# Layout in DRAM of the split q and k of two attention stages: loads by head, one store in place of four

## The reference, cut to what matters

```python
# self attention, 16 heads of 16 features, T = 256
q, k = apply_rotary(q), apply_rotary(k)
weights = softmax(einsum('bhqd,bhkd->bhqk', q, k) * SCALE)
# cross attention: two softmaxes of half heads (8 features), S = 120 keys
a1 = softmax(einsum('bhtd,bhsd->bhts', q1, k1) * SCALING)
a2 = softmax(einsum('bhtd,bhsd->bhts', q2, k2) * SCALING)
attn = einsum('bhts,bhsd->bhtd', a1 - lam * a2, v) * (1 - LAMBDA_INIT)
```

## Time and profile before

| | before |
|---|---|
| median of three runs | 1919.88 us |
| the profiled execution | 1924.67 us |
| its span in the profile | 1922.6 us |
| mean granted clock of TensorE | 0.946 |
| TensorE busy, weight loads | 88%, 62% |
| VectorE, ScalarE, GpSimd busy | 68%, 56%, 45% |
| DMA packets | 312,751, 302.79 MB |
| queue of SP's transfers, share of 16 engines | 62.0% |

### The profile page before, as it was taken

One profiled execution on the slowest core, in us unless ns is written; L12 is line 12 of the kernel. 1 busy time (PEld: TensorE's weight loads), 2 busy tenths in 40 slices (PEclk: granted clock), 3 DMA queues, 4 the chain that ended last, 5 costly groups with the idle time before them and its releaser, 6 DMA issues. The chain is left out here.

```text
span 1922.6 us, 43658 instructions
## 1 busy us (share of the span) xinstructions
PE 1690.0 (88%) x14562; PEld 1183.5 (62%) x14562; DVE 1310.4 (68%) x2959; ACT 1083.8 (56%) x1701; POOL 858.5 (45%) x788
## 2 busy tenths in 40 slices
PE   3789999999999997889989989999898749999985
PEld 2566667666666665555556555555555438888774
DVE  3566776777666775668888887988888544444275
ACT  1466666666666665567777777777776501111244
POOL 4567776777666742211212111111211005887565
PEclk6899999999999999899999999999998759999998
DMA  5577767776777666566655566566664326887686
GB/s 121 132 190 184 193 168 196 188 188 170 195 189 188 169 172 144 123 119 132 139 132 128 127 129 125 136 133 141 135 125 87 90 59 177 197 195 196 178 292 218
DMA packets 312751, 302.79 MB, mean 157 GB/s; under 512 B 68842, under 2 KB 289836, under 8 KB 303304
## 3 DMA queue, kind: packets, MB, share of 16 engines
q1 hardware_dynamic: 302408, 288.66, 62.0%
q0 software_dynamic: 10240, 12.81, 3.9%
HBM read 188.36 MB, written 112.00 MB: 156 GB/s over the span
## 5 line engine op out<-in xcount | busy, mean ns | idle before, releaser
L1340 DVE TENSOR_REDUCE att_nmax<-self_p_mx 128x2 f32<-128x512 f32 x512 | 328.8, 686 | 203.3 <-PE self_p_mx L629 202.8
L1430 DVE TENSOR_REDUCE att_cross_nmax<-self_p_mx 128x8 f32<-128x960 f32 x256 | 294.4, 1150 | 86.5 <-PE self_p_mx L829 85.4
L1074 ACT ACTIVATE att_probs<-self_p_sc 128x1024 f32<-128x1024 f32 x256 | 261.3, 1021 | 98.5 <-PE self_p_sc L617 96.2
L1167 ACT ACTIVATE att_probs<-self_p_sc 120x1024 f32<-120x1024 f32 x256 | 261.9, 1023 | 65.4 <-PE self_p_sc L811 64.5
L629 PE MATMUL self_p_mx<-att_k_stack,att_q_stack 96*128 96x256 bf16 x1024 | 160.8, 277 | 54.5 <-DMA att_k_stack<-self_k_parts 49.2
L847 PE MATMUL self_p_pv<-att_probs,att_v_aug 120*32 120x256 f32 x2048 | 172.3, 410 | 0.0
L617 PE MATMUL self_p_sc<-att_q_stack,att_k_stack 99*128 99x256 bf16 x1024 | 158.5, 278 | 11.4 <-ACT att_probs L1074 10.0
L829 PE MATMUL self_p_mx<-att_k_stack,att_q_stack 48*128 48x120 bf16 x2048 | 101.2, 220 | 70.6 <-DMA att_k_stack<-cross_k_parts 37.9
L1683 POOL TENSOR_SCALAR att_cross_var_eps<-att_cross_mv 128x2 f32<-128x2 f32 x32 | 7.2, 226 | 332.3 <-DVE att_cross_mv L1536 289.7
L1697 POOL TENSOR_TENSOR att_qk_rest<-att_qk,att_parts 128x752 f32<-128x752 f32 x32 | 51.8, 1619 | 214.3 <-ACT att_parts L1200 214.3
L629 PEld LDWEIGHTS self_p_mx<-att_k_stack,att_q_stack 96*128 96x128 bf16 x1024 | 96.0, 98 | 82.9 <-DMA att_k_stack<-self_k_parts 35.3
(11 more groups left out here) (180 smaller groups left out, 3682.4 us busy)
## 6 DMA issues: line engine op xcount, KB each, us to landing
att_q_stack<-self_q_parts SPq DMA_DIRECT2D x64, 256.0 KB, 5.7
expert_sums<-att_zeros SPq DMA_DIRECT2D x64, 256.0 KB, 8.7
att_q_stack<-cross_q_parts SPq DMA_DIRECT2D x128, 128.0 KB
ffn_w<-in_ffn_w SPq DMA_DIRECT2D x64, 256.0 KB
ffn_m_sb<-expert_sums SPq DMA_DIRECT2D x32, 512.0 KB, 6.0
self_q_parts<-att_parts SPq DMA_DIRECT2D x32, 384.0 KB
self_k_parts<-att_parts SPq DMA_DIRECT2D x32, 384.0 KB
att_k_stack<-self_k_parts SPq DMA_DIRECT2D x32, 384.0 KB, 7.9
```

The source lines that it names most:

```text
L1074: act.activation(probs[:, g % 4, :], p_sc[:, :, :].rearrange("p b n -> p (b n)"), ACT.Exp, scale=SCALE).then_inc(s_exp, 1)
L1167: act.activation(probs[0:KEYS, g % 4, :], p_sc[0:KEYS, :, :].rearrange("p b n -> p (b n)"), ACT.Exp, scale=C_SCALE).then_inc(c_exp, 1)
L1340: dve.tensor_reduce(nmax[:, M.slot, :, m], p_mx[:, m % 2, :].rearrange("p (c k) -> p c k", c=TC), AX_X, ALU.max, negate=True).then_inc(s_r ...
L1430: dve.tensor_reduce(cnmax[:, M.slot, :, :, 2 * m:2 * m + 2].rearrange("p c e h -> p e h c"), p_mx[:, :, 0:4 * KEYS].rearrange("p e (x k) - ...
```

## The change

The self parts in DRAM get rows of `T + 32` = 288 values (576 B) of which 256 are used, so that the 16 head rows of one feature don't follow each other without a gap, and the stack loads name the head as a dimension of its own: 16 pieces of 512 B per row. The cross parts of q and k of both half heads lie in one tensor whose rows are the 752 values (1504 B) of a partition of `cparts`: one transfer stores all of them, and the stack loads take 512 B (q) or 240 B (k) of each row. The counts on `c_pw` go from 64 to 16 a batch. Number, order and bytes of the stack loads stay as they were.

```diff
--- before.py
+++ after.py
@@ -141,8 +141,9 @@
     y_rows = y_out.rearrange("(b c p) d -> b p c d", p=P, c=TC)
     moe_rows = [m[0:N_TOK, :].rearrange("(b c p) d -> b p c d", p=P, c=TC) for m in moe]
     res_rows = res_out.rearrange("(b c p) d -> b p c d", p=P, c=TC)
-    q_dram = nc.dram_tensor("self_q_parts", [3, NP, 2, P, T], BF16, kind="Internal").ap()
-    k_dram = nc.dram_tensor("self_k_parts", [3, NP, 2, P, T], BF16, kind="Internal").ap()
+    PITCH = T + 32
+    q_dram = nc.dram_tensor("self_q_parts", [3, NP, 2, P, PITCH], BF16, kind="Internal").ap()
+    k_dram = nc.dram_tensor("self_k_parts", [3, NP, 2, P, PITCH], BF16, kind="Internal").ap()
 
     C_LAGS = 7
     KEYS = ctxT_in.shape[1]
@@ -176,8 +177,7 @@
     cres_rows = res_out.rearrange("(b c p) d -> b p c d", p=P, c=TC)
     ctxT_rows = ctxT_in.rearrange("(b f p) n -> b p f n", f=FC, p=P)
     cy_rows = z_out.rearrange("(b c p) d -> b p c d", p=P, c=TC)
-    cq_dram = nc.dram_tensor("cross_q_parts", [3, E, NP, P, T], BF16, kind="Internal").ap()
-    ck_dram = nc.dram_tensor("cross_k_parts", [3, E, NP, P, KEYS], BF16, kind="Internal").ap()
+    c_dram = nc.dram_tensor("cross_parts", [3, NP, P, QW + KW], BF16, kind="Internal").ap()
 
     with ExitStack() as ctx:
         def sb(label, shape, dt=F32):
@@ -462,11 +462,12 @@
 
                     if past(B.n, 3):
                         sp.wait_ge(s_sc, NG * (B.n - 2))
-                    q_src = q_dram[B.slot].rearrange("t c (d h) n -> (t c d) (h n)", h=NH)
-                    k_src = k_dram[B.slot].rearrange("t c (d h) n -> (t c d) (h n)", h=NH)
+                    q_src = q_dram[B.slot].rearrange("t c (d h) n -> (t c d) h n", h=NH)
+                    k_src = k_dram[B.slot].rearrange("t c (d h) n -> (t c d) h n", h=NH)
                     for is_q, row, src_row, m in STACK_LOADS:
                         stack, src = (q_stack, q_src) if is_q else (k_stack, k_src)
-                        sp.dma_start(stack[row:row + m, B.slot, :], src[src_row:src_row + m, :])\
+                        dst = stack[row:row + m, B.slot, 0:NH * T].rearrange("p (h n) -> p h n", h=NH)
+                        sp.dma_start(dst, src[src_row:src_row + m, :, 0:T])\
                           .then_inc(s_st[B.slot], 16)
                 if R.on:
                     sp.wait_ge(s_yb, R.n + 1)
@@ -495,7 +496,7 @@
                     if past(A.n, 3):
                         sp.wait_ge(s_st[A.slot], 16 * N_ST * A.turn)
                     for z, dram in enumerate((q_dram, k_dram)):
-                        sp.dma_start(dram[A.slot].rearrange("t c p n -> p (t c) n"),
+                        sp.dma_start(dram[A.slot][:, :, :, 0:T].rearrange("t c p n -> p (t c) n"),
                                      parts[:, z, :, :, :].rearrange("p t c n -> p (t c) n")).then_inc(s_pw[A.slot], 16)
                 if O.on:
                     sp.wait_ge(s_y, O.n + 1)
@@ -540,7 +541,7 @@
                         sp.wait_ge(c_sum, S.n - 2)
                     sp.dma_start(x_res[:, S.slot, :, :], cres_rows[S.n]).then_inc(c_res_in[S.slot], 16)
                 if B.on:
-                    n_pw = held(sp, 64 * (B.turn + 1))
+                    n_pw = held(sp, 16 * (B.turn + 1))
                     sp.wait_ge(c_wts, 16)
                     sp.wait_ge(c_pw[B.slot], n_pw)
 
@@ -548,13 +549,13 @@
                         sp.wait_ge(c_ones, B.n + 1)
                     if past(B.n, 3):
                         sp.wait_ge(c_sc, NGR * (B.n - 2))
+                    by_row = c_dram[B.slot].rearrange("t (d h) n -> (t d) h n", h=NH)
                     for e in range(E):
-                        q_src = cq_dram[B.slot][e].rearrange("t (d h) n -> (t d) (h n)", h=NH)
-                        k_src = ck_dram[B.slot][e].rearrange("t (d h) n -> (t d) (h n)", h=NH)
                         for is_q, row, src_row, m in C_STACK_LOADS:
-                            stack, src, n = (q_stack, q_src, T) if is_q else (k_stack, k_src, KEYS)
-                            sp.dma_start(stack[e * HALF + row:e * HALF + row + m, B.slot, 0:NH * n],
-                                         src[src_row:src_row + m, :]).then_inc(c_st[B.slot], 16)
+                            stack, at, n = (q_stack, e * T, T) if is_q else (k_stack, QW + e * KEYS, KEYS)
+                            dst = stack[e * HALF + row:e * HALF + row + m, B.slot, 0:NH * n]
+                            sp.dma_start(dst.rearrange("p (h n) -> p h n", h=NH),
+                                         by_row[src_row:src_row + m, :, at:at + n]).then_inc(c_st[B.slot], 16)
                 if R.on:
                     sp.wait_ge(c_y, R.n + 1)
                     sp.dma_start(cy_rows[R.n][:, :, 0:DM], y_sb[:, R.slot, :, :]).then_inc(c_stored[R.slot], 16)
@@ -582,11 +583,8 @@
 
                     if past(A.n, 3):
                         sp.wait_ge(c_st[A.slot], 16 * C_N_ST * A.turn)
-                    for e in range(E):
-                        sp.dma_start(cq_dram[A.slot][e].rearrange("t p n -> p t n"),
-                                     cparts[:, :, e * T:(e + 1) * T]).then_inc(c_pw[A.slot], 16)
-                        sp.dma_start(ck_dram[A.slot][e].rearrange("t p n -> p t n"),
-                                     cparts[:, :, QW + e * KEYS:QW + (e + 1) * KEYS]).then_inc(c_pw[A.slot], 16)
+                    sp.dma_start(c_dram[A.slot].rearrange("t p n -> p t n"), cparts[:, :, :])\
+                      .then_inc(c_pw[A.slot], 16)
 
             run_both(sp, step, cross_step, n_batches, LAGS, C_LAGS)
             sp.wait_ge(c_ahead, 16 * (len(ahead) + P // n_batches))
@@ -1193,7 +1191,7 @@
                 act.wait_ge(c_qe, 2 * (A.n + 1))
 
                 if past(A.n, 1):
-                    act.wait_ge(c_pw[last.slot], 64 * (last.turn + 1))
+                    act.wait_ge(c_pw[last.slot], 16 * (last.turn + 1))
                 else:
                     for p in range(3):
                         act.wait_ge(s_pw[p], 32 * len(range(p, n_batches, 3)))
```

## The result

The change makes the kernel slower: 2041.76 us (median of four runs) against 1922.99 us for the kernel before beside it, a ratio of 1.0623 (1.0559 to 1.0688). The forecast was 1900 us with a range up to 1928 us, so the result lies far outside it. The profiled execution took 2042.25 us.

What follows compares the result with a forecast made beforehand. TensorE nearly bounds both attention stages, its remaining idle time being waits for stack loads. Cross gains 23 us, self loses 4: 19 off 1919.9 gives 1901, stated as 1900 us; own range 1885 to 1915, full range 1843 to 1928.

Steps and rivals of the forecast that it cites:

- Where the time is limited: Both attention stages: TensorE waits for stack loads; 1 us saved gives 1 us a cross step, 0.5 a self step.
- the 97 us: Waits for stack loads at L629 (self, 42.6 us) and L829 (cross, 54.4 us): the most the change can give back.
- The cross store: Cross stage: four stores of the parts become one, landing after 3.9 us; gain 1.2 us a step, bounds 0.9 and 1.6.
- Loads in pieces: Stack loads: the partitions' shared rate also meets pieces, so self loads gain nothing; 0.3 us loss taken over two steps.
- The comparison of engine times: Self loads: 16 pieces of 512 B cost an engine 459 ns, under a row's 0.52 or 1.00 us at the shared rates.
- The prediction's last sentence: Stack loads: the forecast is wrong above all if a load's rate depends on the packet and not on the partitions.
- The 240 B pieces: Cross k loads: pieces take 0.3 us a step off the cross gain, bounds 0 and 1.6.
- SP's own time: SP's issues: up to 0.9 us more for 7 self loads, 1.7 for 14 cross; costed at nothing, covered by earlier loads' data.
- Rival 3: Both stages: pieces read from DRAM cost twice a store's price, 57 ns, making loads late; 1969 us, chance 0.13.
- Rival 1: Stack loads: large packets are slow in themselves, so pieces remove nearly all load waits; 1845 us, chance 0.2.
- Rival 2: Cross stage: another wait, VectorE's reduction, takes the place and the step stays; 1919 us, no change, chance 0.17.

Runs made afterwards that it cites:

- whole rows spread: Kernel before with whole-row stack loads, each load's rows two partitions apart and the pairs of parts reordered, both stages: 1890.89 us, ratio 0.9885.
- the tiny loads: Kernel before with a tiny load ahead of each of the 8 cross q loads only: 1939.17 us, ratio 1.0136.
- the issues doubled: Kernel before with a tiny load (16 x 8 B) ahead of each of the 14 cross stack loads: 1980.13 us, ratio 1.0323.
- Issuing on two engines: Cross part of the change alone, with ScalarE issuing the second half head's seven loads and SP the other seven: 2094.78 us, ratio 1.0941.
- spread change: The whole change (pieces, one cross store) with the rows of each load two partitions apart: 1897.11 us, ratio 0.991.

## Why the prediction was wrong

**Where the time is limited:** right. TensorE's waits for the loads, a cross step that is one way round and a self step that is two steps long. The self stage's 1.25 us a group against 0.67 us a step shows the two; 3.15 us times 32 in the cross stage the one. But the 97 us that the change could at most give back was too much. With whole rows spread, L629 and the load of weights before it wait 5 us for the loads between 60 and 700 us in place of 43, L829 11 us between 800 and 1440 us in place of 44, and the kernel gains 25 us.

**The cross store:** right. Store to first load falls by 1.45 us (forecast 1.4 and 1.2 net, bounds 0.9 and 1.6), the landing takes 3.4 us (forecast 3.9). In time it was worth 14 to 18 us with the pieces in place, and nothing once the rows were spread.

**Loads in pieces, "pieces to the same partitions from the same engines meet it again":** this is the step that failed. The sentence takes the shared rate of four neighbouring partitions for a property of the partitions alone, to be met again by any packet. That something is shared there was right; that it doesn't depend on the packet was assumed, and the stack loads of before had no packet smaller than 3840 B to show it by. It does depend: 101 to 85 GB/s on 16 rows. (The 131 and 254 GB/s of the earlier trace rows have more than one transfer in them; alone, 16 and 32 rows get 101 and 204.) The comparison of engine times (459 ns against 520 and 1000) was of the wrong resource: it shows that the engine is not late, and the engine was not what was late. In the self stage the step cost 24 us where 4 were set down, in the cross stage the pieces of both, their issues included, cost 109 us. The prediction's last sentence named this case as what it would be wrong by; the runs show that the rate depends on both, the packet and the partitions.

**The 240 B pieces:** the third of a microsecond was too little. The k pieces cost 21 us alone, 0.7 us a step (1.0 from first load to restart), inside the bounds given (0 to 1.6); but the bound was set for k, and the larger loss was in the 512 B pieces of q, which carry two thirds of the bytes and had been given no cost.

**SP's own time:** mis-sized. Forecast 1.7 us more for the 14 loads, from the nearest rows of transfers that differ in packets; measured 4.6. The row was of the wrong kind: the cost comes with a third dimension in the access pattern, not with the number of packets. The store of q beside it, which the earlier trace rows leaves out, has as many packets as that of k and takes 380 ns:

```profile
L498 SPq DMA_DIRECT2D self_q_parts<-att_parts x32: 372/380/1212, 27.9 to 698.8; - x32
```

That the cover holds ("still under way") is barely right: 10.1 us and 2.1 are less than the 12.6 that the loads took. With nearly equal issuing q pieces cost 76 us and the tiny loads 23.

**Missing altogether: the clock.** Longer waits were mostly followed by a lower granted clock. Before, most waits are short (0.81 and 0.70 us in the earlier trace rows) and leave the clock; after, they average 3.4 us and most are followed by 0.50. The length of the wait alone does not decide it: with the issues doubled, seven waits of 2.6 to 2.8 us left the clock at 1.00. The lower clock costs 0.6 us of the 3.15 us a step, and 20 us of the 119.

**The rivals.** Rival 3 (slower, 1969 us) had the right sign and side, and its loss of 0.6 us a step by 128 pieces in the narrow loads was the right place; its price of 57 ns for a piece in DRAM is not what the runs show, since spread pieces cost almost nothing. Nor do they show its misaligned starts: spread, or on 32 rows, 512 B pieces with such starts are as fast as whole rows, or nearly (239 and 247 GB/s). Rival 1's large packets are not slow in themselves: they are slow on neighbouring partitions. Rival 2's end state is what spreading the rows brings.

**How the chances went wrong.** The case that one shared rate gets worse with smaller packets was not among the rivals. Rival 3 was argued from the price at the source, so the counter-evidence there (28.7 ns a piece) seemed to bear on it; it didn't bear on the destination. And the two terms put at nothing, the issue and the pieces on narrow loads, both lay on the path that the same text had found to be one way round.

**What stays open:** why small packets use the shared rate worse on few partitions, and how the 3.8 us divide exactly: the pieces of q and k cost 97 us apart and 109 together. The rates by themselves were taken with one kind of load in the queue; how the two kinds mix there was not tried. Issuing on two engines parted nothing; what parts issuing from data is the changed kernel with its rows spread.

## What to carry to other kernels

Before cutting a load into smaller pieces, ask how many groups of four partitions it reaches, and whether that rate, not the engine's time for a packet, is what the transfer waits for; where it is, put the rows two partitions apart (119 us of loss became a gain of 19 to 25 us here). Count an extra dimension, or a step in the partitions, as 0.2 to 0.3 us of the issuing engine's time for each transfer, and check the row of issues against the data: the last issue and what follows it (here 4.9 us) must still end first. And price the clock behind a wait of TensorE that grows: here most waits of under 2 us left it whole, and most of those of 3 us and more were followed by half of it.

## What the runs showed of the hardware

- The issue of a load is 0.30 to 0.42 us for rows in one piece and 0.60 to 0.65 us by itself for rows in 16, 8 or 4 pieces, whatever their number (0.60 to 0.68 in the kernel after). A destination of every second partition costs the same: in the spread kernel the median is 628 ns. Both together cost little more, 684 ns in the spread change. The lines, before and spread: engine, transfer, count, shortest/median/longest ns.

```profile
L556 SPq DMA_DIRECT2D att_q_stack<-cross_q_parts x256: 281/307/1980, 730.6 to 1462.2; - x128
...
L557 SPq DMA_DIRECT2D att_q_stack<-cross_q_parts x192: 513/628/1187, 716.9 to 1433.7; - x192
```

- Packets of 512 B lose 16% on 16 neighbouring partitions and nothing on 32; 240 B lose 16% and 23%. Row starts 64 B off a multiple of 8 KB cost nothing (145 and 146 GB/s). To give each piece of k a place of 256 B changed nothing in the k groups (18.7 and 18.6 us for three); alone, it cost on 16 rows (85 to 66 GB/s) and helped on 32 (152 to 178).
- The share of the DMA engines reads over 1 while small packets are under way, at 85 GB/s on 16 rows (1.25) as at 208 on 32 (1.20): a high share is then no sign of much work.
- After one wait of 3.4 us TensorE ran 5 to 6 us at half its clock (1139.9 to 1145.5 us).
